# ScalarE in place of VectorE copies the value sums of the two 16-head attentions out of PSUM

## The reference

```
# block 0: keys are the 1024 tokens (causal) and the 77 context tokens
scores = einsum('bthd,bshd->bhts', q, k) * scale
scores = where((j >= t) | (j <= i), scores, -inf)
attn_out = einsum('bhts,bshd->bthd', softmax(scores), v)
# block 3: keys are the 77 context tokens alone
scores = einsum('bqhd,bkhd->bhqk', q, k)
out = einsum('bhqk,bkhd->bqhd', softmax(scores / sqrt(256)), v)
```

## Time and profile before

| | |
|---|---|
| Median of 3 runs | 1566.38 us (1565.34 to 1569.76) |
| Profiled execution, first to last instruction | 1562.7 us |
| First 16-head attention | 117.0 to 427.6 us of it |
| Last 16-head attention | 1340.0 to 1429.7 us of it |
| Mean granted PE clock | 0.937 of full speed |

### The profile page before, as it was taken

One profiled execution on the slowest core, in us unless ns is written; L12 is line 12 of the kernel. 1 busy time (PEld: TensorE's weight loads), 2 busy tenths in 40 slices (PEclk: granted clock), 3 DMA queues, 4 the chain that ended last, 5 costly groups with the idle time before them and its releaser, 6 DMA issues.

```text
span 1562.7 us, 21716 instructions
## 1 busy us (share of the span) xinstructions
PE 1342.9 (86%) x7242; PEld 768.5 (49%) x7242; DVE 1070.4 (68%) x2665; ACT 749.0 (48%) x1048; POOL 530.2 (34%) x448
## 2 busy tenths in 40 slices
PE   5869998999779979888999989799998788788896
PEld 3513333333268856544444356344443677445796
DVE  4677777777565357776567768675767888676654
ACT  5405555555767445623334435223443734345664
POOL 3001111111241042306776622178865257001212
PEclk8959999999989989989999989799999889899998
DMA  7952333330000000464422305724400020730001
GB/s 252 263 124 46 58 58 58 58 58 2 7 22 1 1 1 34 135 196 95 95 47 49 114 32 185 194 49 95 95 28 1 27 35 24 161 64 3 1 1 54
DMA packets 79849, 110.29 MB, mean 71 GB/s; under 512 B 16576, under 2 KB 55674, under 8 KB 77946
## 3 DMA queue, kind: packets, MB, share of 16 engines
q1 hardware_dynamic: 79737, 108.91, 28.0%
HBM read 70.55 MB, written 37.80 MB: 69 GB/s over the span
## 4 chain that ended last, share of the span: by engine, by line
PE 40%; POOLq 19%; DVE 17%; issue 11%; ACT 6%; DVEq 3%; SPq 2%; DMA 2%; POOL 1%; ACTq 0%
POOLq L1085 18%; PE banks L1556 5%; PE banks L1196 5%; PE banks L1541 5%; PE banks L1138 4%; PE banks L2107 3%; DVE max_parts L1370 3%; PE banks L1171 3%; PE banks L571 2%; DVE mask_rows L1366 2%; PE banks L2137 2%; DVE scratch L1366 2%; PE banks L1149 1%; PE banks L2655 1%; DMA stacks<-neg_max_parts 1%
## 5 line engine op out<-in xcount | busy, mean ns | idle before, releaser
L1331 ACT ACTIVATE x_feat<-banks,key_bias 128x1024 f32<-128x1024 f32 x160 | 176.2, 1114 | 263.7 <-PE banks L1178 203.7
L1084 POOL TENSOR_TENSOR x_feat<-x_feat 128x1024 f32<-128x1024 f32 (+1 forms) x112 | 242.7, 2167 | 95.9 <-ACT x_feat L1331 87.4
L1138 PE MATMUL banks<-stacks 128*128 128x512 f32 (+4 forms) x640 | 230.3, 407 | 37.9 <-DVE max_parts L1359 13.6
L1196 PE MATMUL banks<-x_feat,v_group 128*32 128x512 f32 (+4 forms) x1312 | 230.9, 568 | 8.6 <-ACT x_feat L1331 4.8
L1331 ACT ACTIVATE x_feat<-banks 128x1024 f32<-128x1024 f32 (+2 forms) x224 | 178.8, 840 | 121.8 <-PE banks L1171 120.0
L1138 PEld LDWEIGHTS banks<-stacks 96*128 96x128 bf16 (+1 forms) x640 | 77.2, 139 | 229.1 <-DVE max_parts L1359 92.5
L1108 POOL TENSOR_SCALAR_AFFINE_SELECT x_feat<-x_feat 128x256 f32<-128x256 f32 x128 | 53.7, 420 | 291.4 <-ACT x_feat L1331 290.0
L1171 PE MATMUL banks<-stacks 99*128 99x512 bf16 (+3 forms) x512 | 131.2, 346 | 24.2 <-ACT x_feat L1331 13.9
L1359 DVE CUSTOM_DVE_ANT_0 scratch<-banks,mask_rows 128x512 f32<-128x512 f32 x128 | 88.2, 689 | 49.4 <-PE banks L1138 49.3
L1177 PE MATMUL banks<-stacks 128*128 128x512 f32 x256 | 110.9, 433 | 9.5 <-DMA stacks<-neg_max_parts_r 9.5
L1541 PE MATMUL banks<-stacks 128*128 128x512 f32 x384 | 101.0, 401 | 9.3 <-DVE stacks L1523 8.5
(11 more groups left out here) (295 smaller groups left out, 2470.7 us busy)
## 6 DMA issues: line engine op xcount, KB each, us to landing
stacks<-q_parts_r SPq DMA_DIRECT2D x18, 512.0 KB, 12.1
stacks<-k_parts_r SPq DMA_DIRECT2D x18, 512.0 KB, 14.0
q_parts_r<-stacks SPq DMA_DIRECT2D x16, 512.0 KB, 3.0
k_parts_r<-stacks SPq DMA_DIRECT2D x16, 512.0 KB, 3.5
v_group<-v SPq DMA_DIRECT2D x14, 512.0 KB, 14.5
stacks<-q_parts SPq DMA_DIRECT2D x16, 384.0 KB, 5.2
w_even<-in_w SPq DMA_DIRECT2D x4, 1024.0 KB, 6.6
stacks<-q_parts SPq DMA_DIRECT2D x16, 256.0 KB, 5.5
```

The source lines that it names most:

```text
L1084: e.tensor_tensor(total, total, p, ALU.add)
L1138: m = e.matmul(PS[:, bank, at:at + wide], q[0:rows, h, qt * P:(qt + 1) * P], keys[0:rows, h, k0:k0 + wide], start=True, stop=True, skip_gr ...
L1196: m = e.matmul(PS[w * h:w * (h + 1), bank, t.q0:CH], V[:, h, :], PB[:, t.index % 2, h // 2, h % 2, 0:CH - t.q0], start=t.first, stop=t.las ...
L1331: e.activation(dst, PS[:, 2 * (st % 2):2 * (st % 2) + 2, 0:CH - t.q0], ACT.Exp, scale=A.scale, bias=bias).then_inc(s.p_ready, 1)
```

## The change

VectorE's list loses item "C" in the 16-head attentions, and ScalarE takes the copy as an ACTIVATE with function Copy, at places of its own. The copy of half 0 follows the exponentials of tile `nt0`, the first key tile of half 1. The copy of half 1 follows the exponentials of tile 0 of the next group; that of the last group follows the last exponentials. Each waits for its value products (`pv_tile`) and for the transposes that read the buffer before it (`chunk_ready`). VectorE gets a drain ahead of the reciprocal. PE, GpSimd and SyncE keep their lists, and no DMA is added. The attentions with 64-wide heads keep the copy on VectorE.

```diff
     def attention_scalar(e, A):
         s = A.s
+        turned = {(r + dg, c): n for r in range(A.n + 1) for items in numbered(A, 0, r) for w, dg, c, n, _ in items if w == "E"}
+
+        def copy_sums(g, c):
+            e.wait_ge(s.pv_tile, g * A.nt + (A.nt if c else A.nt0))
+            if (g, c) != (0, 0):
+                e.wait_ge(s.chunk_ready, turned[(g, 0) if c else (g - 1, 1)] + 1)
+            e.activation(OT[:, :], PS[:, 4 + c, :], ACT.Copy).then_inc(s.copied, 1)
+
         def run(i, r):
+            if r == A.n and A.dh == 16:
+                copy_sums(A.n - 1, 1)
...
+                if A.dh == 16 and t.index == A.nt0:
+                    copy_sums(g, 0)
+                if A.dh == 16 and t.index == 0 and g > 0:
+                    copy_sums(g - 1, 1)
...
             if A.dh == 16:
+                e.drain()
                 reciprocal(o[:, :, :, 16], g, c)
...
+                    if w == "C" and A.dh == 16:
+                        continue
                     if w == "C":
                         last = A.nt0 if k == 0 else A.nt
                         e.wait_ge(s.pv_tile, (g + dg) * A.nt + last)
-                        e.tensor_copy(OT[:, :], PS[:, 4 + k if A.dh == 16 else 4, :]).then_inc(s.copied, 1)
+                        e.tensor_copy(OT[:, :], PS[:, 4, :]).then_inc(s.copied, 1)
```

## The result

| | before | changed |
|---|---|---|
| Median, 20 runs each | 1567.01 us (1564.55 to 1575.04) | 1574.31 us (1565.61 to 1583.07) |
| Ratio, 95% interval | | 1.0035 (1.0019 to 1.005) |
| Profiled execution, span | 1562.7 us | 1579.7 us |
| First attention, first to last reciprocal | 285.2 us | 292.7 us |
| Last attention, first to last reciprocal | 63.5 us | 61.2 us |

Scaled to the 1566.38 us that the forecast started from, the ratio gives 1571.9 us; the forecast was 1570.0 in 1565 to 1574. The changed kernel's own median, 1574.31, is 0.3 us above that range. The ratio stands just over the line of 0.3%, which the forecast had put at 31%, against 62% for "the same".

A forecast was written before the change was run, and what follows sets the result against it. No engine was taken as full: TensorE and VectorE hand two chunk banks to and fro, and the later one counts. First attention +6.0 and last -2.5, with rounding +3.6 on 1566.38, gave 1570.0 us, range 1565.0 to 1574.0.

The forecast's parts named there:

- Drains and late transposes: First attention: drains ahead of reciprocals, +1.1 us mid-group and +0.4 at group starts; transposes held by ScalarE's copy, +4.2 us.
- Copy ahead of the table load: First attention's last group: half 0's copy on ScalarE stands ahead of a table load TensorE waits behind, +0.5 us.
- Last copy: End of the first attention: TensorE idles 0.91 us for VectorE's last copy; ScalarE's shorter one gives -0.2 us.
- Half 0 on VectorE: First attention, seven groups: TensorE itself sets when the next chunk comes, so removing VectorE's copy of half 0 gives 0.
- ScalarE's price: First attention, half 0: ScalarE's copy takes 0.59 us, ends some 0.25 us ahead of the next scores, cost 0.
- The drain: First attention, ahead of each reciprocal: 0.16 us in a group's middle (+1.1 in all), 0.07 at its start (+0.4).
- The late transposes: First attention, groups 1 to 6: half 1's copy behind tile 0's exponentials delays transposes 0.70 us each, +4.2 us.
- The last attention: Half 1's transposes come earlier, -0.25 us in five groups (-1.3); the last two groups give -1.2; sum -2.5 us.
- The dear drain: Rival: each of 13 drains on the path costs 0.27 us, sum +5.6, 1572.0 us, slower; chance 20%.
- VectorE as the bound: Rival: everyone follows VectorE, so each copy with chunks behind it gives 0.60 us; -7.8, 1558.6 us, faster; chance 7%.
- the stall made good: Rival: half 1's stall is taken back inside the group, so 4.2 us fall away; 1565.8 us, the same; chance 10%.
- Table loads: Rival: Copy and Exp each fetch a table on ScalarE, 64 x 1.28 = 82 us, 1648 us; chance 1%.

The follow-up runs named there:

- second profile: The unchanged program of the changed kernel, measured and profiled again against the kernel before: ratio 1.0012 (0.999 to 1.0034), median 1570.52 us.
- both cures: Changed kernel with half 1's copy ahead of the exponentials and two reciprocal tiles instead of drains: ratio 0.9981, again 0.9971, against the kernel before.

## Why the prediction was right, step by step

The stages of the changed kernel's second profile, which has the kernel before's clock there, can be set beside the sum term by term.

| term | forecast, us | measured, us |
|---|---|---|
| Drains and late transposes, first attention (141.57 to 396.50 before) | +5.5 of +5.7 | +5.6 |
| Copy ahead of the table load | +0.5 | +0.4 |
| Last copy | -0.2 | -0.1 |
| First attention | +6.0 | +5.9 |
| Last attention, groups | -1.3 | -1.2 |
| Last attention, last groups | -1.2 | -1.1 |
| Both | +3.6 | +3.6 |
| All executions, means at the same clock | | +3.5 (2.6 to 4.5) |

In the first row one of the seven drains in a group's middle, 0.16 us, lies ahead of the first reciprocal, where the ruler doesn't reach.

**Half 0 on VectorE.** Right: its removal is worth 0.03 us a group, for the reason given. TensorE takes 1.00 us for the value product without a copy beside it and took 0.99 with one.

**ScalarE's price.** Right: the copy out of a bank takes 0.60 us (0.59 forecast from the row of another line), and 0.26 us of idle were left behind it (0.25).

**The drain.** Right in both parts, 0.07 at a group's start and 0.17 in its middle (0.16). The Trainium skill, "VectorE: DVE Perf Modes", section "The DRAIN you can't avoid", says that the next instruction does not start until the pipe is empty; the prediction had inferred from it that an explicit drain would add next to nothing (1568.5 us). The trace disagrees with that: 0.24 us a group with the drain put in alone, and 0.25 back with it taken out. The section also says that an instruction that is not held starts earlier, which the prediction left out and with which the trace agrees: the reciprocal starts at 180.99, before the accumulator read in front of it ends at 181.07.

**The late transposes.** Right: +0.70 forecast, 0.69 between exponential and transposes, 0.73 in the group's time. Nothing took it back, and moving the copy ahead of the exponentials gave back all of it, so the place is the cause.

**The last attention.** Right in sign, and in size partly by luck. A group gains 0.20 instead of 0.25, and at the first group the gain is 0.40: the two misses make up for each other in the sum of the five. The drain, which I had put into VectorE's waits, adds 0.07 a group there when it stands alone (9.49 against 9.42), but nothing beside half 1's move: with two reciprocal tiles in its place the groups still take 9.22.

**The rivals.** The dear drain, VectorE as the bound, and the stall made good are each refuted by one experiment: 39.32, 39.29 and 40.05 us a group. Table loads were not added: the traces show 27 in the kernel before and 27 in the changed one.

**What the forecast missed** is not a term of its sum but its yardstick. I took 0.3% as what a measurement can tell. With single times that range over some 17 us (1565.6 to 1583.1 for this kernel) and follow the granted clock, the ratio of the first measurement came out at 1.0035 and that of the second at 1.0012, for one program whose stages cost 3.6 us, 0.23%. Both intervals hold 1.0023.

## What to carry to other kernels

An engine that is busy 80% of a stage need not be its bound: look at who idles beside the instruction to be moved, and if it is that very engine, taking work off it buys idle time. When work is moved to an engine with room, its place in that engine's order decides: here the same copy cost 0.7 us a group behind two exponentials, and nothing ahead of them, where the engine waited anyway. And count the guard that the move needs; a second small tile cost nothing where a drain cost 0.24 us a group.

## What the hardware showed that I had not expected

TensorE's granted clock behind the first attention took two courses in the same program: 10 us at 1.2 GHz in one profile of the changed kernel, 24 in the other, and the first attention left as before was followed by the long one too. The long one costs 2.0 us behind the attention (19.2 in place of 17.2 us to the next projection's first product), where TensorE waits for much of the time, and is not by itself the 12 us that the two profiles differ by between the attentions. Over the twelve profiles that part, whose TensorE instructions no run changes, takes 938.6 to 950.4 us with 116 to 149 us of it at 1.2 GHz in several pieces, and its time grows by 0.3 us for each microsecond more at 1.2 GHz (correlation 0.91). The times of single executions follow the mean granted clock by 0.8 us for each 0.001. What sets the course these runs don't tell; several profiles of one kernel, and the stages in place of the whole, told the changes apart where 20 timed runs of each had left 0.2 to 0.5%.

The last attention gave 4.8 us with both cures where the change alone gave 2.3. The single cures say how much of it is each one's: half 1's copy ahead of the exponentials takes it from 61.2 to 59.4 us, two reciprocal tiles alone leave it at 61.2, and the two together give 58.7. So 1.8 us come from the copy's place, and taking the drain out is worth 0.7 only on top of that. In the groups' starts with both cures (1380.72) TensorE is released by VectorE's maxima again, as before the change, and not by ScalarE's copy.
